# Layernorm by TensorE ahead of the first tile of an adjacency kernel, its first load issued earlier, and row blocks marked whole or not at all

## The chip, the cores and the metric

The kernel runs on one core of a Trainium2 chip. The metric is the device time of one launch in microseconds (us), the median of three runs. Beside it stands one profiled execution, whose span (first to last instruction) is what the trace divides up. Engines are called PE (TensorE; PEld is its weight load), DVE (VectorE), ACT (ScalarE), POOL (GpSimd) and SP (SyncE, which here only issues DMAs).

## The reference

```python
N, D_IN, D_OUT = (4096, 64, 64); MAX_NEIGH = 100; DECAY = 0.5
h = jnp.maximum(_layernorm(x, axis=-1), 0.0)        # x: 4096 x 64
support = h @ weight
mask = (adj != 0)                                   # adj: 4096 x 4096
rank = jnp.cumsum(mask, axis=1)
deg = rank[:, -1:]
k = jnp.minimum(deg, 100.)
pos = rank - (deg - k)
w = mask * jnp.where(pos > 0, 0.5 ** (k - pos), 0.0)
out = x + (w @ support + bias)
```

Every row of `adj` gives its nonzero columns weights that halve from the last nonzero backwards; those weights times a 4096 x 64 matrix, plus bias and x, are the result. `adj` is 64 MB in fp32 and is nearly all the data.

## The kernel before

**Tiles.** Row r of `adj` belongs to partition r // 32 and to tile r % 32, so there are 32 tiles of 128 rows. Column j belongs to partition j // 32 and to step t = j % 32 once PE has turned it. Tiles are taken in 18 units (`SIZES`): four of one tile (0, 1, 2, 17), fourteen of two.

**What a unit costs.** POOL loads a tile from fp32 to bf16 (`load`, L200 to 206, 1 MB in SBUF each) into a ring of 7 buffers. DVE turns it into a byte mask (`mask`, L310), adds halves of the mask (L316, three times, L344 the last) and scans the sums (L353), which gives for each run of columns how many nonzeros stand behind it. PE then begins a chain in PSUM (`base`, L549) and goes through the steps (`count`, L561 and L563), ACT turns each step's exponents into bit patterns of bf16 powers (`weigh`, L266), and PE multiplies them with the support rows into an accumulator (`product`, L570, 192 columns, since the support stands as three bf16 parts). DVE at the end adds the three parts, x and bias (`add_low`, `add_middle`, `add_high`), and SP stores.

**Marked or plain.** `MARKS[u]` says how many tiles of a unit are marked. A marked tile costs PE two matmuls a step and chain (`diag_own` and `diag_past`) and DVE nothing more. A plain tile costs PE one (`diag_step`), and DVE a maximum (`floor`, L362) and a difference (`differ`, L369) over each batch of 8 steps, on which that batch's products wait. 20 of the 32 tiles are marked in both kernels.

**Order.** Nothing schedules at run time. PE, ACT and DVE each go through slots g = 0, 1, 2 and so on, and do in each what tables place there: unit u begins in slot `STARTS[u]` (its base), counts in the next 8 or 16 slots, and its products come `LAGS[u]` slots behind. Chain c = u % 3 has one PSUM bank. A count of slot g+1 waits for the ACT instruction of slot g of its chain. DVE places the masks of a unit 9 and 7 slots ahead of its base, the halvings 6, 5 and 4, the scans 3 and 2 ahead. Each engine works in program order, so whatever waits holds all behind it.

**Layernorm.** Ahead of the slots DVE and POOL center x (`center`, L403 and L223), ACT squares (`square`, L239, into the last load buffer), DVE sums the squares (`square_sums`, L408), and between the DVE work for tiles 0 to 2 come the reciprocal deviation (L412 to 427) and the product with it (`normalize`, L432). PE turns the rows (`turn_h`, L514), ACT applies the Relu (L248), PE multiplies by the weight (`make_support`, L524), and ACT and PE split the result in three bf16 parts (`part`, L255; `take_off`, L532) in slots 5 to 11.

## Time and profile before

| | |
|---|---|
| median of 3 runs | 231.36 us (231.02 to 233.29) |
| the profiled execution | 232.5 us, of which the span is 230.1 us |
| PE busy | 201.8 us, 88% of the span, 2768 matmuls |
| DVE busy | 197.7 us, 86%, 227 instructions |
| ACT busy | 163.7 us, 71%, 303 instructions |
| DMA | 36.11 MB moved, about 216 GB/s from 6 to 165 us |
| first matmul | at 18.0 us |

A matmul's duration in the trace is its latency (its end is modelled), so the pace of PE is read from the starts of consecutive matmuls, or from how many there are in a stretch. The share of the DMA engines is that of 16 engines together. A number in square brackets at a row's end is the idle time ahead of it and what ended it.

### The profile page before, as it was taken

How to read it: one execution, taken by the hardware profiler on the slowest of the kernel's cores; microseconds unless marked ns; L12 is line 12 of the kernel's file. 1: busy time of each engine (PE TensorE's matmuls, PEld its weight loads, DVE VectorE, ACT ScalarE, POOL GpSimd, SP SyncE). 2: the span in 40 equal slices, each digit the busy share in tenths (PEclk: the TensorE clock that was granted, in tenths of full speed). 3: DMA queues.
4: the chain of work that ended last, by engine and by line, in shares of the span. 5: the costliest groups of instructions: out<-in, count | busy, mean ns of one | idle time of the engine just before them, and what ended most of it. 6: DMA issues, size and time to landing. Idle time of an engine off the chain costs nothing.

```text
span 230.1 us, 6364 instructions
## 1 busy us (share of the span) xinstructions
PE 201.8 (88%) x2768; PEld 196.3 (85%) x2768; DVE 197.7 (86%) x227; ACT 163.7 (71%) x303; POOL 26.0 (11%) x53
## 2 busy tenths in 40 slices
PE   0005898899999999999999999999999899899994
PEld 0004885899999999999999999999999789899993
DVE  1799999997799989999979999969999999677053
ACT  2203489767877988878887878887889798787610
POOL 8921000411000010110010001000000000000000
PEclk9999999999999999999999999999999999999999
DMA  5999999999999999999999999999700000000001
GB/s 182 227 214 194 215 216 216 216 216 216 212 215 216 215 214 211 215 219 216 215 215 219 218 214 220 212 218 218 158 20 3 11 3 14 0 14 3 11 14 29
DMA packets 8074, 36.11 MB, mean 157 GB/s; under 512 B 1648, under 2 KB 3440, under 8 KB 3952
## 3 DMA queue, kind: packets, MB, share of 16 engines
q0 software_dynamic: 4608, 33.56, 70.1%
q1 hardware_dynamic: 3136, 2.10, 3.5%
q8 instruction: 22, 0.36, 0.6%
q10 hardware_dynamic: 304, 0.07, 0.1%
q14 instruction: 4, 0.03, 0.0%
HBM read 68.22 MB, written 1.05 MB: 301 GB/s over the span
## 4 chain that ended last, share of the span: by engine, by line
PE 71%; DVE 17%; issue 4%; DMA 4%; ACT 3%; POOL 1%; POOLq 0%
PE acc L570 31%; PE chain L563 22%; PE chain L561 13%; DVE masks L310 6%; DMA adj_b<-in_adj 4%; DVE part L316 3%; DVE powers L369 2%; PE acc L524 2%; ACT support L255 2%; DVE powers L362 2%; PE chain L549 1%; PE acc L514 1%; ACT powers L266 1%; DVE later L353 1%; DVE sums L344 1%
## 5 line engine op out<-in xcount | busy, mean ns | idle before, releaser
L266 ACT ACTIVATE powers<-chain 128x512 int16<-128x512 f32 (+1 forms) x282 | 152.3, 568 | 39.3 <-PE chain L563 31.3
L570 PE MATMUL acc<-support,powers 128*128 128x192 bf16 x1024 | 167.5, 246 | 2.8 <-issue 1.3
L563 PE MATMUL chain<-diag_own,masks 128*128 128x128 bf16 x640 | 125.6, 231 | 0.0
L561 PE MATMUL chain<-diag_past,masks 128*128 128x128 bf16 x596 | 118.5, 224 | 3.0 <-ACT powers L266 2.9
L570 PEld LDWEIGHTS acc<-support,powers 128*128 128x128 bf16 x1024 | 101.1, 102 | 4.5 <-DVE powers L369 1.7
L563 PEld LDWEIGHTS chain<-diag_own,masks 128*128 128x128 fp8e3 x640 | 91.0, 147 | 0.0
L561 PEld LDWEIGHTS chain<-diag_past,masks 128*128 128x128 fp8e3 x596 | 84.8, 145 | 5.0 <-ACT powers L266 4.7
L310 DVE TENSOR_SCALAR masks<-adj_b 128x4096 uint8<-128x4096 bf16 x32 | 72.9, 2279 | 3.8 <-DMA adj_b<-in_adj 3.8
L563 PE MATMUL chain<-diag_step,masks 128*128 128x128 bf16 x384 | 62.2, 220 | 0.0
L563 PEld LDWEIGHTS chain<-diag_step,masks 128*128 128x128 fp8e3 x384 | 52.1, 145 | 0.0
L206 POOL DMA_DIRECT2D adj_b<-in_adj x32 | 18.7, 585 | 116.3 <-DVE masks L310 111.8
L369 DVE TENSOR_TENSOR powers<-powers 128x2048 bf16<-128x2048 bf16 (+1 forms) x20 | 28.5, 1423 | 0.0
L353 DVE TENSOR_TENSOR_SCAN later<-sums 128x257 bf16<-128x257 uint8 (+1 forms) x32 | 22.9, 721 | 0.4
L549 PE MATMUL chain<-diag_base,later 128*128 128x128 bf16 x68 | 7.1, 226 | 18.0 <-DVE later L353 18.0
L362 DVE TENSOR_SCALAR powers<-powers 128x2304 int16<-128x2304 int16 (+3 forms) x20 | 17.2, 862 | 6.2 <-ACT powers L266 6.2
L549 PEld LDWEIGHTS chain<-diag_base,later 128*128 128x128 bf16 x68 | 4.8, 103 | 18.0 <-issue 18.0
L316 DVE TENSOR_TENSOR part<-masks 128x2048 uint16<-128x2048 uint16 (+1 forms) x18 | 19.9, 1104 | 0.2
L379 DVE TENSOR_TENSOR sum_a<-acc,x_sb 128x128 f32<-128x128 f32 (+1 forms) x18 | 4.9, 272 | 12.0 <-PE acc L570 12.0
L344 DVE TENSOR_TENSOR sums<-part 128x512 uint16<-128x512 uint16 (+1 forms) x18 | 11.9, 663 | 0.5
L316 DVE TENSOR_TENSOR part<-part 128x1024 uint16<-128x1024 uint16 (+1 forms) x16 | 10.5, 654 | 0.1
L255 ACT ACTIVATE support<-acc 128x512 bf16<-128x512 f32 x12 | 6.8, 620 | 1.9 <-PE acc L524 1.9
L394 DVE TENSOR_REDUCE row_sum<-x_sb 128x16 f32<-128x1024 f32 x2 | 2.4, 1220 | 5.4 <-DMA x_sb<-in_x 5.4
(45 smaller groups left out, 53.0 us busy)
## 6 DMA issues: line engine op xcount, KB each, us to landing
adj_b<-in_adj POOLq DMA_DIRECT2D x32, 1024.0 KB, 30.3
x_sb<-in_x SPq DMA_DIRECT2D x2, 512.0 KB, 4.7
out<-x_sb SPq DMA_DIRECT2D x14, 64.0 KB, 2.6
out<-x_sb SPq DMA_DIRECT2D x4, 32.0 KB, 9.3
w<-in_L_gnn_weight ACTq DMA_DIRECT2D x2, 16.0 KB, 4.6
bias_b<-in_L_gnn_bias ACTq DMA_DIRECT2D x1, 32.0 KB, 4.5
```

The costliest lines, as they stand in the source:

```text
L206: pool.dma_start(adj_b[:, n % LOADS, :], adj_t[n]).then_inc(adj_loaded[n % LOADS], 16)
L266: nc.scalar.activation(powers[:, c, b, cols].bitcast(i16), chain[c][:, cols], ACT.Relu, bias=(MAX_NEIGH + 1) * STEP).then_inc(powers_ready ...
L310: nc.vector.tensor_scalar(masks[:, (n + SHIFT) % RING, :], adj_b[:, n % LOADS, :], 0.0, 1.0, ALU.not_equal, ALU.mult).then_inc(mask_ready, 1)
L316: return nc.vector.tensor_tensor(outs, at[:, :, 0:length], at[:, :, length:2 * length], ALU.add).then_inc(done, 1)
L344: nc.vector.tensor_tensor(runs_of(sums, sums_4, u)[:, :, 0:h * P], at[:, :, :, 0], at[:, :, :, 1], ALU.add).then_inc(sums_ready, 1)
L353: nc.vector.tensor_tensor_scan(runs_of(later, later_4, u)[:, k, ::-1], two[:, 0, ::-1], two[:, 1, ::-1], (OWN + STEP) / STEP if k < MARKS[ ...
L362: nc.vector.tensor_scalar(bits, bits, STEP, None, ALU.max).then_inc(floored[c], 1)
L369: nc.vector.tensor_tensor(before, before, after, ALU.subtract).then_inc(weights_ready[c], 1)
L549: last = nc.tensor.matmul(chain[c][:, at:at + P], behind[:, hs - 1 - h], diag_base[:, :], start=(k + h == 0), stop=False, skip_group_check ...
L561: nc.tensor.matmul(chain[c][:, at:at + P], column(n, t + 1), diag_past[:, :], start=False, stop=False, skip_group_check=True)
L563: return nc.tensor.matmul(chain[c][:, at:at + P], column(n, t), diag_own[:, :] if marked else diag_step[:, :], start=False, stop=True, ski ...
L570: return nc.tensor.matmul(acc[u % ACCS][:, k * 3 * D:(k + 1) * 3 * D], powers[:, u % FLIGHT, s + 1 if k < MARKS[u] else s, at:at + P], sup ...
```

## The change

1. **Loads.** POOL issues load 0 ahead of the constants and no longer centers half of x. The load ring has 8 buffers and the mask ring 12 (7 and 10 before); room for this comes from placing `cen` and `h_t` in the power buffer of chain 2 and the squares in that of chain 1. x comes in two halves as before, which now interleave in runs of four rows of 64 numbers (1 KB) and not of eight (2 KB).
2. **Layernorm.** PE runs 40 matmuls that nothing reads, and then, ahead of slot 0, turns the centered rows, not the normalized ones. ACT both squares and Relus them out of PSUM, and PE sums the squares by a matmul with two columns of ones. `make_support` works on relu(x - mean) in slot 1, into the four accumulator banks, and DVE multiplies by the reciprocal deviation there (`scale`), since relu(c r) = r relu(c) for r > 0. `square_sums` and `normalize` go. The three parts are taken in slots 1 to 6.
3. **DVE order.** `variance` comes behind `mask(1)`; the bias is added in four quarters at slots 15, 24, 50 and 72; the first scan of a unit comes in the slot of the last halving.
4. **Tables.** `MARKS`, `STARTS` and `LAGS` are new. The units with plain tiles were 4, 6, 7, 9, 10, 12, 13, 16 (one each) and 14, 15 (two); now they are 5, 16 (one) and 8, 11, 14, 15 (two).

`SIGNED` is empty, so the new `signs` and its branch in `mask` issue nothing.

```diff
-    LOADS = 7
-    RING = 10
+    LOADS = 8
+    RING = 12
-    MARKS = [1, 1, 1, 2, 1, 2, 1, 1, 2, 1, 1, 2, 1, 1, 0, 0, 1, 1]
-    STARTS = [0, 5, 10, 15, 22, 28, 33, 39, 45, 50, 56, 62, 67, 73, 79, 84, 90, 96]
-    LAGS = [14, 10, 8, 11, 11, 11, 11, 11, 11, 11, 11, 11, 11, 11, 11, 11, 11, 8]
+    MARKS = [1, 1, 1, 2, 2, 1, 2, 2, 0, 2, 2, 0, 2, 2, 0, 0, 1, 1]
+    STARTS = [0, 5, 7, 13, 22, 29, 34, 39, 46, 51, 56, 63, 68, 73, 80, 85, 90, 97]
+    LAGS = [7, 7, 8, 11, 11, 11, 11, 11, 11, 11, 11, 11, 11, 11, 11, 11, 11, 7]
...
-                if n == LOADS - 1:
-                    pool.wait_ge(sq_sum_ready, 2)
...
             nc.gpsimd.memset(w2[:, :], 0.0).then_inc(w2_zeroed, 1)
+            load(0)
             for m in (ident_f, minus, diag_own, diag_past, diag_step, diag_base):
...
-            pool.wait_ge(mean_ready, 2)
-            nc.gpsimd.tensor_tensor(half_of(cen, 1), half_of(x_sb, 1), spread(mean, 1),
-                                    ALU.subtract).then_inc(cen_ready[1], 1)
...
+            def scale(i):
+                dve.wait_ge(ln_step, 6)
+                dve.wait_ge(support_ready, i + 1)
...
+                nc.vector.tensor_tensor(block_of, block_of, of_block.unsqueeze(3).to_broadcast([P, RUNS, 2, D]),
+                                        ALU.mult).then_inc(scaled[i], 1)
...
+            def keep_warm(times):
+                for _ in range(times):
+                    nc.tensor.matmul(chain[0][:, 0:P], minus[:, :], diag_step[:, :], start=True, stop=True,
+                                     skip_group_check=True)
+            def sum_squares(i):
+                pe.wait_ge(sq_ready, i + 1)
+                for q in range(4):
+                    t = 8 * q + 6 - 2 * i
+                    last = nc.tensor.matmul(sq_sum[:, t:t + 2], sq_t[:, 4 * i + q, :], pair_sum[:, :],
+                                            start=(q == 0), stop=True, skip_group_check=True)
...
             pe.wait_ge(consts_ready, 6)
+            keep_warm(40)
+            turn_h(0)
+            turn_h(1)
+            pe.wait_ge(consts_ready, 7)
+            sum_squares(0)
+            turn_h(2)
+            sum_squares(1)
+            turn_h(3)
+            sum_squares(2)
+            sum_squares(3)
             for g in range(SLOTS):
...
+                if g == 1:
+                    make_support(0)
+                    make_support(1)
+                    make_support(2)
+                    make_support(3)
...
-                    if u >= 3 and to == 3:
+                    if u >= 3 and to == 4:
                         scan(u, 0)
```

On DVE, at the start of the program, these rows stood before (row sums of x, the first mask, the squares' sums):

```order
L394 TENSOR_REDUCE row_sum<-x_sb 128x2x8 x2
L398 TENSOR_SCALAR mean<-row_sum 128x2x8 x2
L403 TENSOR_TENSOR cen<-x_sb,mean 128x2x512
L408 TENSOR_REDUCE sq_sum<-adj_b 128x2x8
L310 TENSOR_SCALAR masks<-adj_b 128x4096
L316 TENSOR_TENSOR part<-masks 128x1024
L408 TENSOR_REDUCE sq_sum<-adj_b 128x2x8
L344 TENSOR_TENSOR sums<-part 128x512
L353 SCALAR_TENSOR_TENSOR later<-sums 128x513
L412 TENSOR_SCALAR var_eps<-sq_sum 128x32
L310 TENSOR_SCALAR masks<-adj_b 128x4096
```

In the changed kernel there stand (L445 is `center`, which writes where the powers will be; L450 is `variance`, which reads a chain's bank):

```order
L436 TENSOR_REDUCE row_sum<-x_sb 128x4x4
L445 TENSOR_TENSOR powers<-x_sb,mean 128x4x256
L440 TENSOR_SCALAR mean<-row_sum 128x4x4
L445 TENSOR_TENSOR powers<-x_sb,mean 128x4x256
L351 TENSOR_SCALAR masks<-adj_b 128x4096
L357 TENSOR_TENSOR part<-masks 128x1024
L385 TENSOR_TENSOR sums<-part 128x512
L394 SCALAR_TENSOR_TENSOR later<-sums 128x513
L351 TENSOR_SCALAR masks<-adj_b 128x4096
L450 TENSOR_SCALAR var_eps<-chain 128x32
```

Nothing of layernorm stands between the first mask and its scan any more, both halves are centered on DVE, and the variance has moved behind the second mask.

On ACT, from the square root on, the rows of the changed kernel are these (L262 is `root`, L298 `weigh`, L275 `part`):

```order
L262 ACTIVATE std<-var_eps 128x32
L298 ACTIVATE powers<-chain 128x512
L275 ACTIVATE support<-acc 128x4x2x64 x2
L298 ACTIVATE powers<-chain 128x512
L275 ACTIVATE support<-acc 128x4x2x64 x2
L298 ACTIVATE powers<-chain 128x512
L275 ACTIVATE support<-acc 128x4x2x64 x2
```

Before, four `weigh` came directly behind the root, and no part ahead of the sixth:

```order
L243 ACTIVATE std<-var_eps 128x32
L266 ACTIVATE powers<-chain 128x512 x4
L248 ACTIVATE h_t<-acc 128x512 x2
L266 ACTIVATE powers<-chain 128x512
L255 ACTIVATE support<-acc 128x8x64 x2
L266 ACTIVATE powers<-chain 128x512
```

So the parts now alternate with unit 0's steps from the first step on.

On DVE, where units 14 and 15 (both plain) are at work, the rows before were:

```order
L362 TENSOR_SCALAR powers<-powers 128x4608
L353 SCALAR_TENSOR_TENSOR later<-sums 128x257
L369 TENSOR_TENSOR powers<-powers 128x4096
L379 TENSOR_TENSOR sum_a<-acc,x_sb 128x128
L362 TENSOR_SCALAR powers<-powers 128x8x256
L384 TENSOR_TENSOR sum_b<-acc,sum_a 128x128
L316 TENSOR_TENSOR part<-masks 128x1024
L369 TENSOR_TENSOR powers<-powers 128x8x256
```

and are now:

```order
L403 TENSOR_SCALAR powers<-powers 128x4608
L410 TENSOR_TENSOR powers<-powers 128x4096
L421 TENSOR_TENSOR sum_a<-acc,x_sb 128x128
L426 TENSOR_TENSOR sum_b<-acc,sum_a 128x128
L357 TENSOR_TENSOR part<-masks 128x1024
L431 TENSOR_TENSOR x_sb<-acc,sum_b 128x128
L385 TENSOR_TENSOR sums<-part 128x512
L394 SCALAR_TENSOR_TENSOR later<-sums 128x513
```

The scan between maximum (L362, now L403) and difference (L369, now L410) has moved ahead of them, and unit 13's maximum and difference over 256 columns are gone.

## Rows read from the trace of the kernel before

**Rows 1.** Busy time by stretch: us, each engine's busy us (x instructions), clock, DMA, GB/s
```profile
150.00:160.00 10.00, 10.00 (x150) 10.00 (x148) 8.21 (x12) 8.19 (x15) 0.00 (x0) 1.00 1.04 217
...
180.00:190.00 10.00, 8.55 (x121) 8.26 (x121) 9.90 (x11) 8.21 (x16) 0.00 (x0) 1.00 0.03 8
190.00:200.00 10.00, 9.12 (x133) 8.98 (x132) 8.34 (x11) 8.26 (x15) 0.00 (x0) 1.00 0.03 8
```

**Rows 2.** The chain of work that ended last: start us, us, what
```profile
35.05 2.04 PE acc L524 x16
...
43.18 0.22 PE chain L549 x4
...
73.10 0.22 PE chain L549 x4
...
226.79 0.30 DVE sum_a L379
```

**Rows 3.** Timeline of DVE at the start: start us, us, instruction, idle before
```profile
11.82 2.31 DVE L310 TENSOR_SCALAR masks<-adj_b 128x4096 uint8<-128x4096 bf16 x1 [0.29 <-DMA adj_b<-in_adj]
...
14.78 1.21 DVE L408 TENSOR_REDUCE sq_sum<-adj_b 128x16 f32<-128x1024 f32 x1
...
16.62 1.23 DVE L353 TENSOR_TENSOR_SCAN later<-sums 128x513 bf16<-128x513 uint8 x1
17.76 0.15 DVE L412 TENSOR_SCALAR var_eps<-sq_sum 128x32 f32<-128x32 f32 x1
```

**Rows 4.** Timeline: the first DMA issues of x (SP) and of adj (POOL)
```profile
0.74 1.27 SPq L189 DMA_DIRECT2D x_sb<-in_x  x2
...
3.54 2.27 POOL L206 DMA_DIRECT2D adj_b<-in_adj  x4
```

**Rows 5.** DMA queues, 5 to 6 us: packets, MB, share; q1 moves x, q0 adj
```profile
q1 hardware_dynamic: 165, 0.31, 80.5%
q0 software_dynamic: 7, 0.06, 27.9%
```

**Rows 6.** DMA queues, 61 to 62 us; q1 now stores 32 KB of the output
```profile
q0 software_dynamic: 28, 0.20, 93.8%
q1 hardware_dynamic: 28, 0.01, 5.1%
```

**Rows 7.** Timeline of ACT: the first `weigh`, and two `part`
```profile
19.05 0.60 ACT L266 ACTIVATE powers<-chain 128x512 int16<-128x512 f32 x1 [0.86 <-PE chain L563]
...
39.08 1.13 ACT L255 ACTIVATE support<-acc 128x512 bf16<-128x512 f32 x2
```

**Rows 8.** Timeline of DVE: bias over 2 x 1024 columns, tile 4, tile 10
```profile
32.33 2.35 DVE L438 TENSOR_TENSOR x_sb<-x_sb,bias_b 128x1024 f32<-128x1024 f32 x2
34.72 2.29 DVE L310 TENSOR_SCALAR masks<-adj_b 128x4096 uint8<-128x4096 bf16 x1
...
39.77 1.28 DVE L353 TENSOR_TENSOR_SCAN later<-sums 128x257 bf16<-128x257 uint8 x2
...
62.78 2.29 DVE L310 TENSOR_SCALAR masks<-adj_b 128x4096 uint8<-128x4096 bf16 x1 [1.42 <-DMA adj_b<-in_adj]
```

**Rows 9.** Timeline of PE, slot 19: its first matmuls, and the first of slot 20
```profile
49.25 0.24 PE L570 MATMUL acc<-support,powers 128*128 128x192 bf16 x1
49.33 0.22 PE L561 MATMUL chain<-diag_past,masks 128*128 128x128 bf16 x1
49.39 0.23 PE L563 MATMUL chain<-diag_own,masks 128*128 128x128 bf16 x1
...
51.02 0.24 PE L570 MATMUL acc<-support,powers 128*128 128x192 bf16 x1
```

**Rows 10.** Timeline of DVE at unit 14: maximum, unit 16's second scan, difference
```profile
185.48 1.36 DVE L362 TENSOR_SCALAR powers<-powers 128x4608 int16<-128x4608 int16 x1
186.76 0.69 DVE L353 TENSOR_TENSOR_SCAN later<-sums 128x257 bf16<-128x257 uint8 x1
187.36 2.27 DVE L369 TENSOR_TENSOR powers<-powers 128x4096 bf16<-128x4096 bf16 x1
```

More of the change, by code:

```diff
@@ L216, in _ @@
                                         pattern=[[-1, P]], channel_multiplier=1).then_inc(consts_ready, 1)
-            for n in range(4):
+            nc.gpsimd.affine_select(out=pair_sum[:, :], in_=pair_sum[:, :], compare_op=ALU.is_ge, fill=0.0, base=0,
+                                    pattern=[[-D, 2]], channel_multiplier=1).then_inc(zeroed, 1)
+            pool.wait_ge(zeroed, 8)
+            nc.gpsimd.affine_select(out=pair_sum[:, :], in_=pair_sum[:, :], compare_op=ALU.is_ge, fill=0.0, base=D - 1,
+                                    pattern=[[D, 2]], channel_multiplier=-1).then_inc(consts_ready, 1)
+            for n in range(1, 4):
                 load(n)
@@ L246, in turn_h, with part, signs @@
                 act.wait_ge(h_turned, i + 1)
-                t = 4 * BLOCKS[i]
-                nc.scalar.activation(h_t[:, t:t + 4, :], turned[i % 2][:, :].rearrange("p (a b) -> p a b", a=4),
+                nc.scalar.activation(h_t[:, 4 * i:4 * i + 4, :], turned[i % 2][:, :].rearrange("p (a b) -> p a b", a=4),
                                      ACT.Relu).then_inc(h_t_ready, 1)
-            def part(i, s, ready):
-                act.wait_ge(split_ready, 6 * (i // 2) + 2 * s + i % 2 + 1)
-                t = 8 * BLOCKS[i]
-                nc.scalar.activation(support[:, t:t + 8, s, :], split[i % 2][:, :].rearrange("p (t d) -> p t d", d=D),
-                                     ACT.Copy).then_inc(ready, 1)
+            def part(i, s):
+                if s:
+                    act.wait_ge(part_taken[i], s)
+                else:
+                    act.wait_ge(scaled[i], 1)
+                nc.scalar.activation(steps_of(support[:, :, s, :], i),
+                                     split[i][:, :].rearrange("p (r two d) -> p r two d", two=2, d=D),
+                                     ACT.Copy).then_inc(part_ready[i], 1)
+            def signs(n, j):
+                act.wait_ge(adj_loaded[n % LOADS], 16 * (n // LOADS + 1))
+                if n >= RING:
+                    u = UNIT_OF[n - RING]
+                    act.wait_ge(chain_ready[u % FLIGHT], taken_until(u) + TAKEN[u])
+                at = slice(j * N // PIECES, (j + 1) * N // PIECES)
+                nc.scalar.activation(masks[:, (n + SHIFT) % RING, at].bitcast(i8), adj_b[:, n % LOADS, at],
+                                     ACT.Sign).then_inc(signs_ready, 1)
             def weigh(u, b):
@@ L264, in weigh @@
                 act.wait_ge(chain_ready[c], taken_until(u) + b + 1 - (MARKS[u] == SIZES[u]))
+                if u in (1, 2) and b <= 1:
+                    act.wait_ge(sq_sum_ready if u == 1 else support_ready, 4)
                 cols = slice(0, SIZES[u] * CHAINS[u] * P) if b else plain(u)
@@ L300, in _ @@
                             weigh(u, g - STARTS[u])
+                for n in SIGNED:
+                    if 0 <= g - SIGNED[n] < PIECES:
+                        signs(n, g - SIGNED[n])
+                if g == 1:
+                    part(0, 0)
+                    part(1, 0)
+                if g == 2:
+                    part(2, 0)
+                    part(3, 0)
+                if g == 3:
+                    part(0, 1)
+                    part(1, 1)
+                if g == 4:
+                    part(2, 1)
+                    part(3, 1)
+                if g == 5:
+                    part(0, 2)
+                    part(1, 2)
+                if g == 6:
+                    part(2, 2)
+                    part(3, 2)
         @block.vector
@@ L305, in mask @@
             def mask(n):
+                if n in SIGNED:
+                    dve.wait_ge(signs_ready, PIECES * (1 + sum(m < n for m in SIGNED)))
+                    two = masks[:, (n + SHIFT) % RING, :].bitcast(u16)
+                    nc.vector.tensor_scalar(two, two, 0x0101, None, ALU.bitwise_and).then_inc(mask_ready, 1)
+                    return
                 dve.wait_ge(adj_loaded[n % LOADS], 16 * (n // LOADS + 1))
@@ L453, in _ @@
             scan(0, 0)
+            mask(1)
             variance()
-            mask(1)
             halve_1(1)
             deviation()
+            scale(0)
             halve_2(1)
+            scale(1)
             halve_3(1)
             scan(1, 0)
-            normalize(0)
+            scale(2)
+            scale(3)
             mask(2)
             halve_1(2)
-            normalize(1)
             halve_2(2)
```

192 lines of the change are left out of this document (89 added, 103 removed).

## The prediction

> **What bounds the kernel now.** I read the busy time by stretch first. From 150 to 160 us PE starts 150 matmuls, 15 a us [rows 1]. Elsewhere two things fall out of that pace: 180 to 200 us has 121 and 133 matmuls where 300 would fit [rows 1], so (300 - 254) / 15 = 3.1 us are lost there; and up to about 50 us PE is thin.
>
> Then I read where the slots lie in time, by the bases in the chain of waits: unit 3's base (slot 15) is at 43.18, unit 6's (slot 33) at 73.10, and the last adds begin at 226.79 [rows 2]. The prediction is made in these three pieces.
>
> Then the timeline inside a slot. A product is 0.08 us, a count 0.06 [rows 9]. Slot 19 lasts 51.02 - 49.25 = 1.77 us with 24 matmuls, which are 1.5 us of work [rows 9]. The rest is the round trip: a chain's 12 matmuls (0.80 us) and then about 0.95 us until ACT's result is back. So a slot lasts the greater of PE's work and (matmuls of its busiest chain + 0.95): 1.42 us for a chain with eight counts, 1.75 with four products besides. By this rule the 18 slots from 43.18 to 73.10 should take 29.6 us, and took 29.9.
>
> Last, DMA. Tile 10's mask began only when its load landed, at 62.78 [rows 8]. The adj stream is continuous, so how early it starts and what stands behind it matter.
>
> **The start.** DVE took the first mask at 11.82, when load 0 had landed, and the scan that releases PE began at 16.62 and took 1.23 [rows 3]. The square sum at 14.78 (1.21) in between goes [rows 3]: the scan ends at 16.7, 1.15 earlier than 17.85. I give nothing for issuing load 0 earlier. x was issued at 0.74, adj at 3.54 [rows 4], and from 5 to 6 us x still fills 80% of the engines while adj gets its first 7 packets [rows 5]: x and load 0 together need the engines until about 11.5 whoever goes first. Both ends: nothing, or 1 us for gaps in the x phase that adj fills. The worse end is a rival below.
>
> Centering the second half on DVE costs 1.2 us of DVE, between x's landing and 11.8 us where DVE idled; the transposes, squares and their sums lie in PE's and ACT's idle time ahead of the slots. The 40 matmuls (0.11 us each at the low level of TensorE's clock is 4.3 us, an estimate by doubling the 0.06 of [rows 9]) start when the constants are there, about 4.2 us, and end before the centered rows are ready at about 9. If x is on time they cost nothing; if the clock is up for the first slots they gain little, because those slots are set by ACT, as follows.
>
> **Slots 0 to 12.** The gain of 1.15 is given back at once. `variance` was at 17.76 [rows 3] and is now behind `mask(1)`: 16.7 + 2.25 = 19.0. ACT's root stands ahead of the first `weigh`, so that one is at about 19.4, and was at 19.05 [rows 7]. Behind it ACT waits for `scale(0)`: halving 0.7, the six small operations 1.25, scale about 0.6 (half of a bias instruction of 1024 columns, 2.35 / 2 [rows 8]), so 21.7 us. Its operand is in PSUM; twice that price would put 0.6 us more before each of the first scales, 1 to 2 us in all, and I keep that for the range. PE meanwhile does all of `make_support`, 2 x 2.04 us by [rows 2], until about 22.
>
> From 21.7 ACT has two parts (1.13 [rows 7]) and a `weigh` (0.60 [rows 7]) in each slot, 1.7 us, with two short waits for scales 1 to 3 (0.9 us together). That puts slot 7 at about 31.5. Slots 7 and 8 have unit 0's eight counts and four products (1.75 each), ACT is 0.1 behind in them, slots 9 to 12 are light (1.18 three times, 1.35). Unit 3's base, now slot 13, comes at 31.5 + 3.6 + 4.9 = **40.0**, against 43.18.
>
> A bound from DVE stands just below. Tile 4's mask at 34.72 was 6.3 us ahead of the end of unit 3's scans, 39.77 + 1.28 [rows 8]. Tiles 0 and 10 landed at 11.82 and 62.78 at the latest [rows 3, 8], 5.1 us a load; tile 4's is then there at 32.2 at best, and the base not before 38.5. The early part can't gain more than 4.7.
>
> **Slots 13 to 33.** Unit 6's base is now slot 34, so this piece has 21 slots and not 18. By the rule: slot 13 1.35, slot 14 1.5, nine of 1.42 (unit 3's or 4's eight counts alone), six of 1.75 (slots 24 to 29, unit 3's products beside its counts), three of 1.42 and one of 1.75. That is 32.2 us, for 29.9 before: the earlier start is half spent on more and emptier slots. Unit 6's base comes at 72.2, for 73.10. Again DMA is close: tile 10 can't be masked before 62.78, and mask, three halvings, scan, another mask and scan (2.2 + 1.4 + 0.7 + 0.7 + 0.6 + 2.2 + 1.0) give a base not before 71.6.
>
> **From unit 6's base on.** Before, 226.8 - 73.1 = 153.7. The matmuls left behind it are 892 products and 1280 counts for 902 and 1226: +0.8 us after pricing all. The marks: six units' 12 maxima and 12 differences over one tile become 6 and 6 over two. On DVE that saves the fixed cost of twelve instructions and leaves the elements as they were; it is off the path, and I put it at nothing. What counts is the 3.1 us lost at 180 to 200. There the maximum at 185.48 (1.36) and the difference at 187.36 (2.27) had a scan of 0.69 between them [rows 10], and unit 13's plain tile stood in the same queue. Both are gone; DVE has the difference done before the third slot behind (3.6 us for some 5.4). I take 3.0 of the 3.1 back, and charge 0.5 for units 8 and 11, now plain, where a bias quarter or a halving still stands between the two. 153.7 + 0.8 - 3.0 + 0.5 = 152.0.
>
> **Sum.** 40.0 + 32.2 + 152.0 = 224.2, for 226.8: 2.6 us less of the profiled span of 230.1, which becomes 227.5. The profiled execution took 232.5, the median is 231.36, and I take the difference off the median: **228.8 us**.
>
> **Rivals.** *x is starved by load 0 (slower).* In the first us of [rows 6] 28 packets of each queue went: an adj packet of 8 KB for each of 256 bytes, one by one, in turn. If the turns hold from the moment adj's packets come, now about 2.2 us behind an issue at 1 us (as before from 3.54 to the end of the stretch of [rows 5]), x's 1 KB packets go one to each 0.6 us of an engine. Nearly all of x is still to move then. Against it: at 5 to 6 us x had 165 packets to adj's 7 [rows 5], and the packets of adj began only as x ran out, as if what is already handed to an engine goes first. How much of x is handed over by 3.2 us no row shows. If a third of it isn't, its last 20 packets on each engine take 20 x 0.62 = 12 us, it lands near 16 instead of soon after 6, DVE reaches mask 0 at 19 instead of 11.8, and the end moves by 7: 231.36 + 4.7 = 236. If most isn't, it takes the loads' own time: 250 or more. Decision point: x complete later than 8.5 us, since DVE then reaches mask 0 after 11.8, and each us costs one. The Trainium skill, "DMA: Bandwidth & Descriptors", section "Queues, rings and completion order", says that each DMA engine takes the queues in turn, one packet after another. By that rule x is starved; the trace agrees at 61 us and not at 5 us. Chance 0.28, a third of it for the worst.
>
> *The early gain is given back (no change).* The scales' PSUM price, ACT's alternation, or DVE falling behind on plain units 8 and 11 (floor and difference of two tiles, 3.6 us, ahead of everything else) costs 1.5 us more: 230.3. For it: DVE is busy 9.90 of 10 us where plain units were at work [rows 1]. Against: layernorm's share of DVE shrinks, four instructions of 1.2 us going for one and four scales of 0.6. Chance 0.27.
>
> *The clock and DMA give more.* Adj lands a us earlier by filling x's gaps and slots 1 to 6 run at the round trip, not ACT's pace: base 3 at 39, and no stall late: 227.3. It belongs to the forecast's side.
>
> **Chances.** The forecast, gain of 1 to 4 us, 0.45; the no-change case 0.27; starved 0.28. Predicted 228.8, its own range 226.8 to 230.3. The whole range reaches to the milder starved case: 226.5 to 237; a tenth is left above. About 1% (2.3 us) is what a measurement of this kernel can tell from no change. Faster by more than that needs below 229.05: most of the forecast's own case, 0.45 with the better rival in it; same 0.29; slower 0.26.
>
> **What would show it.** The first mask at 11.5 to 11.9 and x's second row sum ahead of 7.5 us: no starving. A second row sum behind 8.5 us: the rival. The first scan ending at 16.7, the root at 19.1 and the first `weigh` at 19.4. ACT without gaps from 22 to 32. Unit 3's base at 40, unit 6's at 72 with tile 10's mask still waiting for its load. 180 to 200 us with nearly 300 matmuls. The forecast is wrong if unit 3's base is later than 42, or if PE falls under 14 matmuls a us around units 8 and 11.

## The result, and the profile of the changed kernel

| | before | changed |
|---|---|---|
| median | 231.77 us (231.02 to 233.29, 4 runs) | 249.59 us (248.31 to 250.17, 4 runs) |
| ratio to before | | 1.075, 95% interval 1.068 to 1.083 |
| span of the profiled execution | 230.1 us | 247.5 us |
| slot 0 begins on PE | 17.99 us | 40.44 us |
| PE busy, matmuls | 201.8 us, 2768 | 216.1 us, 2900 |
| DVE busy, instructions | 197.7 us, 227 | 192.1 us, 214 |

The forecast was 228.8 us (226.5 to 237.0). The kernel became 7.5% slower, and its time lies above the whole range. The first rival, x starved by load 0, came true, near its worst form ("250 or more").

One correction to what stands ahead of the prediction. It is not 20 of 32 tiles that are marked in both kernels: the new `MARKS` marks 22, so 10 tiles are plain and not 12. The forecast added matmuls for this (1280 counts for 1226 behind unit 6's base; the trace has 1266), but its sentence on DVE was wrong: 20 maxima and 20 differences became 12 and 12, over fewer elements as well. The page of the changed kernel has 1680 counts behind the first step of each unit and base (704 + 656 + 320), before it had 1620 (640 + 596 + 384).

These are rows of the page of the changed kernel: the granted clock in 40 slices, the chain's shares by engine, one group of instructions, and one DMA issue (x, with its median time from issue to landing):

```profile
PEclk9955555999999999999999999999999999999999
...
PE 83%; DMA 11%; ACT 3%; DVE 1%; issue 1%; SPq 0%
...
L436 DVE TENSOR_REDUCE row_sum<-x_sb 128x16 f32<-128x1024 f32 x2 | 2.4, 1220 | 23.7 <-DMA x_sb<-in_x 23.7
...
x_sb<-in_x SPq DMA_DIRECT2D x2, 512.0 KB, 15.0
```

DVE's two row sums waited 23.7 us for x, and x took 15.0 us in the median of its halves. All later reading starts from that. Next, parts of the chain of work that ended last (start, duration, what):

```profile
1.49 26.31 DMA x_sb<-in_x
...
27.82 1.22 DVE row_sum L436
...
30.23 1.12 PE spare L567 x4
...
37.37 3.21 PE chain L575 x16
40.58 0.45 PE chain L609 x4
41.02 0.43 PE chain L623 x4
41.45 4.86 PE acc L583 x32
```

It begins with the load of x, goes over the second row sum to PE's turns and square sums (L567, L575), and only at 40.58 to the first base. DVE in the same stretch (start, duration, instruction, idle before):

```profile
27.82 1.22 DVE L436 TENSOR_REDUCE row_sum<-x_sb 128x16 f32<-128x1024 f32 x1 [19.21 <-DMA x_sb<-in_x]
...
31.43 2.29 DVE L351 TENSOR_SCALAR masks<-adj_b 128x4096 uint8<-128x4096 bf16 x1
...
35.20 1.23 DVE L394 TENSOR_TENSOR_SCAN later<-sums 128x513 bf16<-128x513 uint8 x1
...
40.61 0.19 DVE L450 TENSOR_SCALAR var_eps<-chain 128x32 f32<-128x32 f32 x1 [2.00 <-PE chain L575]
```

The second row sum stood at 6.62 us before. Load 0 had landed at about 10 us, but tile 0's mask still began only at 31.43, because it stands behind the centering in DVE's program order. Then I looked at the packets. Of the DMA queues, q1 moves x and q0 adj (packets, MB, share of 16 engines); first from 3 to 4 us, then from 4 to 5:

```profile
q1 hardware_dynamic: 361, 0.36, 101.5%
q0 software_dynamic: 6, 0.05, 24.8%
```

```profile
q0 software_dynamic: 26, 0.21, 102.0%
q1 hardware_dynamic: 11, 0.01, 1.8%
```

Within one us x fell from 361 packets to 11. When adj's first packet began, at 3.89 us, 485 of x's 1024 data packets had begun, so about 34 were left on each of the 16 engines. From 12 to 13 us it was still one for one, and the last of x came in at 27.4 us. The stretch from 12 to 13:

```profile
q0 software_dynamic: 18, 0.15, 85.3%
q1 hardware_dynamic: 19, 0.02, 7.3%
```

Windows of the changed kernel (columns as in [rows 1]):

```profile
20.00:30.00 10.00, 0.00 (x0) 0.00 (x0) 2.18 (x2) 0.00 (x0) 0.00 (x0) 0.50 1.05 224
...
150.00:160.00 10.00, 10.00 (x151) 10.00 (x150) 9.71 (x12) 8.21 (x15) 0.72 (x2) 1.00 1.01 211
...
200.00:210.00 10.00, 10.00 (x146) 9.86 (x145) 8.88 (x10) 9.02 (x17) 0.00 (x0) 1.00 0.03 8
210.00:220.00 10.00, 10.00 (x147) 9.92 (x146) 7.04 (x9) 9.58 (x18) 0.00 (x0) 1.00 0.03 8
```

From 20 to 30 us nothing ran on PE or ACT. Late in the kernel the pace of nearly 15 a us holds; 200 to 220 us is the work of 180 to 200 in the kernel before, shifted by the late start. So the loss is all at the start. PE's timeline says the same: slot 13 begins at 60.72, slot 34 at 92.47, and the last adds come at 244.16. From slot 13 to 34 it took 31.75 us and from there to the last adds 151.7, within 0.5 us of the forecast's 32.2 and 152.0.

### The profile page after: what moved, and what is told of

It reads as the page before. It is cut to its first block, busy times and chain, and to the rows that moved or that the text cites. A ratio compares the mean times of both kernels' runs of the same rounds, so it can differ in the third digit from the quotient of the medians.

```text
span 247.5 us, 6684 instructions
## 1 busy us (share of the span) xinstructions
PE 216.1 (87%) x2900; PEld 209.8 (85%) x2900; DVE 192.1 (78%) x214; ACT 161.7 (65%) x301; POOL 29.3 (12%) x55
## 4 chain that ended last, share of the span: by engine, by line
PE 83%; DMA 11%; ACT 3%; DVE 1%; issue 1%; SPq 0%
PE acc L630 35%; PE chain L623 25%; PE chain L621 15%; DMA x_sb<-in_x 11%; PE chain L575 3%; PE acc L583 2%; ACT support L275 2%; PE chain L609 2%; ACT powers L298 1%; PE spare L567 1%; PE chain L567 1%; DVE row_sum L436 0%; DVE powers L445 0%; SPq L204 0%; DVE sum_a L421 0%
## 5 line engine op out<-in xcount | busy, mean ns | idle before, releaser
L298 ACT ACTIVATE powers<-chain 128x512 int16<-128x512 f32 (+1 forms) x278 | 150.4, 572 | 38.0 <-PE chain L623 35.9
L623 PE MATMUL chain<-diag_own,masks 128*128 128x128 bf16 x704 | 132.0, 227 | 0.0
L621 PE MATMUL chain<-diag_past,masks 128*128 128x128 bf16 x656 | 125.2, 222 | 0.8 <-ACT powers L298 0.5
L623 PEld LDWEIGHTS chain<-diag_own,masks 128*128 128x128 fp8e3 x704 | 98.3, 146 | 0.0
L621 PEld LDWEIGHTS chain<-diag_past,masks 128*128 128x128 fp8e3 x656 | 92.1, 145 | 3.5 <-ACT powers L298 3.2
L623 PE MATMUL chain<-diag_step,masks 128*128 128x128 bf16 x320 | 49.0, 220 | 0.0
L623 PEld LDWEIGHTS chain<-diag_step,masks 128*128 128x128 fp8e3 x320 | 43.0, 144 | 0.0
L219 POOL DMA_DIRECT2D adj_b<-in_adj x32 | 24.3, 764 | 130.2 <-DVE masks L351 129.2
L403 DVE TENSOR_SCALAR powers<-powers 128x4608 int16<-128x4608 int16 (+3 forms) x12 | 13.4, 1114 | 21.4 <-ACT powers L298 21.4
L410 DVE TENSOR_TENSOR powers<-powers 128x4096 bf16<-128x4096 bf16 (+1 forms) x12 | 23.2, 1931 | 0.2
L436 DVE TENSOR_REDUCE row_sum<-x_sb 128x16 f32<-128x1024 f32 x2 | 2.4, 1220 | 23.7 <-DMA x_sb<-in_x 23.7
L567 PE MATMUL spare<-ident_f,powers 128*128 128x128 f32 x8 | 2.2, 432 | 21.0 <-DVE powers L445 21.0
L567 PEld LDWEIGHTS spare<-ident_f,powers 128*128 128x128 f32 x8 | 1.6, 241 | 21.2 <-DVE powers L445 21.2
L557 PE MATMUL chain<-diag_step,minus 128*128 128x128 bf16 x40 | 4.4, 313 | 4.8 <-POOL minus L230 4.8
```

What stands on the lines that cost most here:

```text
L219: pool.dma_start(adj_b[:, n % LOADS, :], adj_t[n]).then_inc(adj_loaded[n % LOADS], 16)
L298: nc.scalar.activation(powers[:, c, b, cols].bitcast(i16), chain[c][:, cols], ACT.Relu, bias=(MAX_NEIGH + 1) * STEP).then_inc(powers_ready ...
L403: nc.vector.tensor_scalar(bits, bits, STEP, None, ALU.max).then_inc(floored[c], 1)
L410: nc.vector.tensor_tensor(before, before, after, ALU.subtract).then_inc(weights_ready[c], 1)
L567: last = nc.tensor.transpose(turned[i % 2][:, q * P:(q + 1) * P], pairs_of(cen[:, :, :], i)[:, q, :], ident_f[:, :])
L621: nc.tensor.matmul(chain[c][:, at:at + P], column(n, t + 1), diag_past[:, :], start=False, stop=False, skip_group_check=True)
```

## The experiments

Theory S (starved): adj's packets take turns with x's, one for one, so x is late by the packets it still has to move on each engine, times the time of an adj packet; all else of the forecast holds. The rival theory: it is not the order of the loads but the new layernorm (longer chain on PE, slower scale, cold clock) or the tables. Unless another is named, an edit is against the changed kernel. Kernel 1 is the kernel of experiment 1, and so on. Ratios are to the kernel before, timed beside it on the same chip; x is complete when its last packet has begun.

**1. Load 0 behind the constants, everything else of the change kept.**

```diff
-            load(0)
...
-            for n in range(1, 4):
+            for n in range(4):
                 load(n)
```

> The changed kernel with load 0 issued behind the constants again, all else as changed. Theory T (load 0's packets take turns with the second half of x, which landed at 27.4 us for about 6): x complete at 6 to 7 us, the first mask at about 12, unit 3's base 20.3 us behind unit 0's, so near 38, unit 6's at 70, and the time 249.6 - 21 + up to 1 = 228 to 230 us. Rival L (layernorm on TensorE ahead of the slots, with the clock at its low level, is what costs): time stays above 238 us, since the prelude's chain from the second row sum to slot 0 is kept (12.6 us in the changed kernel). Rival P (1 KB packets of x are slow in themselves): x lands later than 8 us even so.

Measured: 229.16 us (228.85 to 229.65), ratio 0.984 (0.980 to 0.988), span 227.0. x was complete at 6.20 us. The place of one DMA issue in POOL's order is worth 20 us. The time was inside the expected range, the bases of units 3 and 6 came 2 us later than the 38 and 70 expected. DVE, PE's chain and ACT of this kernel, in three views:

```profile
13.07 2.29 DVE L350 TENSOR_SCALAR masks<-adj_b 128x4096 uint8<-128x4096 bf16 x1 [2.15 <-DMA adj_b<-in_adj]
...
16.85 1.23 DVE L393 TENSOR_TENSOR_SCAN later<-sums 128x513 bf16<-128x513 uint8 x1
...
22.38 0.70 DVE L472 TENSOR_TENSOR acc<-acc,rstd 128x512 f32<-128x512 f32 x1 [0.24 <-PE acc L582]
...
63.04 2.29 DVE L350 TENSOR_SCALAR masks<-adj_b 128x4096 uint8<-128x4096 bf16 x1 [1.22 <-DMA adj_b<-in_adj]
```

```profile
9.49 0.86 PE spare L566 x4
...
16.38 3.20 PE chain L574 x16
19.58 0.45 PE chain L608 x4
```

```profile
20.39 0.23 ACT L261 ACTIVATE std<-var_eps 128x32 f32<-128x32 f32 x1 [2.89 <-DVE var_eps L449]
20.53 0.58 ACT L297 ACTIVATE powers<-chain 128x512 int16<-128x512 f32 x1
23.11 0.60 ACT L274 ACTIVATE support<-acc 128x512 bf16<-128x512 f32 x1 [2.00 <-DVE acc L472]
```

This kernel lets the forecast be read without the starved x. In PE's timeline its bases of unit 3 and unit 6 came at 39.98 and 72.04 (forecast 40.0 and 72.2):

```profile
39.98 0.33 PE L608 MATMUL chain<-diag_base,later 128*128 128x128 bf16 x3
...
72.04 0.34 PE L608 MATMUL chain<-diag_base,later 128*128 128x128 bf16 x3
```

**2. The kernel before, with load 0 ahead of the constants and nothing else.**

```diff
             nc.gpsimd.memset(w2[:, :], 0.0).then_inc(w2_zeroed, 1)
+            load(0)
...
-            for n in range(4):
+            for n in range(1, 4):
```

> The kernel before with nothing changed but load 0 ahead of the constants; x still in 2 KB packets. Theory T, turns packet by packet: the second half of x has 17 packets an engine and not 33, so it lands 17 x 0.65 = 11 us behind 4.1, near 15.5 us, against about 6; the second row sum is at 15.5 and the time 231.8 + 8 to 10 = 240 to 242 us. Rival L or P: x lands near 6 us as before, and the time is within 1 us of 231.8. A turn of equal bytes and not of packets would make x land as late as in the changed kernel, 27 us, and cost 18.

Measured: 242.88 us (242.11 to 243.61), ratio 1.043 (1.038 to 1.047). The old kernel starves as well, so none of the rest of the change is needed for the loss. Its x goes in packets of 2 KB, half as many, and was complete at 17.5 us, 2 us later than I had expected; the time is 0.9 us above the expected 240 to 242. The second row sum, and then the queues from 12 to 13 us:

```profile
18.00 1.22 DVE L395 TENSOR_REDUCE row_sum<-x_sb 128x16 f32<-128x1024 f32 x1 [11.17 <-DMA x_sb<-in_x]
```

```profile
q0 software_dynamic: 21, 0.17, 85.8%
q1 hardware_dynamic: 22, 0.05, 13.2%
```

One packet for one again, whether x's are 1 or 2 KB. The extra delay over 6.2 us is 21.2 us with 1 KB and 11.3 with 2 KB. When adj's first packet began, about 34 KB of x were left on an engine in the changed kernel, and about 40 KB here (20 packets, since 188 of 512 had begun by 4.10 us). More bytes and fewer packets gave the smaller delay, so it goes with the number of x's packets, not with its bytes.

**3. Load 0 first, x in one DMA of 8 KB a partition (8 packets on each engine for 64).**

```diff
-            for f in range(2):
-                sp.dma_start(half_of(x_sb, f), half_of(x.rearrange("(p t) d -> p t d", t=T), f))\
-                  .then_inc(x_loaded[f], 16)
+            sp.dma_start(x_sb[:, :, :], x.rearrange("(p t) d -> p t d", t=T)).then_inc(x_loaded[0], 16)
...
-                dve.wait_ge(x_loaded[f], 16)
+                dve.wait_ge(x_loaded[0], 16)
```

> The changed kernel, load 0 first as changed, but x in one DMA of 8 KB a partition, so 8 data packets an engine for 64. Theory T: its packets start at about 2.2 us and load 0's at 3.8; at most some 4 or 5 packets an engine are left and take turns with adj: x lands at 4 + 5 x 0.9 = 8 us or less, and the time is 228 to 231 us. If adj's load starves x whatever the packets, it lands later than 15 us. Rival L: above 238 us.

Measured: 228.01 us (227.70 to 228.71), ratio 0.980 (0.976 to 0.984), span 225.9. Load 0 is issued as early as in the changed kernel, and x was complete at 5.20 us. With the time between two issues left alone and x put into one DMA of larger packets, 21.6 us of the changed kernel's span are gone. DMA from 4 to 5 us, and DVE:

```profile
q1 hardware_dynamic: 49, 0.37, 87.3%
q0 software_dynamic: 4, 0.03, 16.3%
```

```profile
15.05 1.23 DVE L392 TENSOR_TENSOR_SCAN later<-sums 128x513 bf16<-128x513 uint8 x1
17.03 2.29 DVE L349 TENSOR_SCALAR masks<-adj_b 128x4096 uint8<-128x4096 bf16 x1 [0.75 <-DMA adj_b<-in_adj]
```

The result is the expected one, but its means are not. Adj's first packet came at 4.91 us, 1.0 later than in the changed kernel, and by then all 128 packets of x had begun, so here there were no turns to take. It shows that few large packets avoid the loss; it doesn't test the price of a turn. Why adj's first packet came later isn't shown. The turns themselves are shown by the changed kernel's packets, by 2 and by 8. Whether an early load 0 is worth anything stays open here; 9 and 10 below are for that.

**4. Kernel 1 without `keep_warm(40)`.**

> As the run with load 0 behind the constants, but without the 40 matmuls that nothing reads. If they raise the clock for the transposes and sums: those are at the low level without them, 1 to 2 us longer in the prelude, but this lies in time in which load 0 is awaited, so the total is the same within 0.5 us. If the prelude is on the path, the total is 1 to 2 us more.

Measured: 229.40 us (228.75 to 229.88), ratio 0.985 (0.981 to 0.989), against 0.984: in this kernel the 40 matmuls are worth nothing that can be measured. The row's granted clock differs, the work doesn't. From 12 to 16 us, first kernel 1 with the 40 matmuls, then the one without, then kernel 3, which has them as well:

```profile
12.00:16.00 4.00, 4.00 (x21) 4.00 (x22) 2.90 (x2) 1.54 (x3) 0.34 (x1) 0.50 1.02 213
```

```profile
12.00:16.00 4.00, 4.00 (x21) 4.00 (x21) 2.93 (x2) 1.85 (x4) 0.37 (x1) 1.00 1.01 211
```

```profile
12.00:16.00 4.00, 3.90 (x36) 3.82 (x35) 3.90 (x4) 2.86 (x6) 0.54 (x1) 1.00 0.91 166
```

That is not all that can be said of them. In kernel 1 the 40 matmuls end at 7.4 us and the turns begin at 9.49, and the turns and square sums run at the low level. In kernel 3 they end at 9.3, the turns begin at 9.93, and PE stays at the high level until about 16.5: it begins 36 matmuls in this stretch for 21, its last 16 square sums take 1.90 us for 3.41, and slot 0 begins at 16.33. No run takes the 40 matmuls out of kernel 3, so what they are worth there isn't shown.

**5. Kernel 3 with the marks of before** (20 marked tiles, not 22), starts as changed.

```diff
-    MARKS = [1, 1, 1, 2, 2, 1, 2, 2, 0, 2, 2, 0, 2, 2, 0, 0, 1, 1]
+    MARKS = [1, 1, 1, 2, 1, 2, 1, 1, 2, 1, 1, 2, 1, 1, 0, 0, 1, 1]
```

> Load 0 first, x in one DMA (228.0 us, 0.980 of before), but with the marks of the kernel before: 20 marked tiles and 12 plain for 22 and 10. PE has 60 counts fewer, 3.5 us of its work. Theory M (the new marks pay by keeping DVE ahead where units 14 and 15 are): the plain tiles' maxima and differences cost stalls as in 180 to 200 us before, 3 us, so the total is 0 to 1 us off 228.0 either way, with stalls late and fewer matmuls. Rival W (PE's work alone decides): 3.5 us less, 224.5. Rival D (DVE falls behind throughout): 2 us or more above 228.

Measured: 235.94 us (234.54 to 237.10), ratio 1.017 (1.013 to 1.022), 8 us more than kernel 3, with 60 matmuls fewer on PE (rival D). PE now waits for DVE's differences. From the waits (engine, line, waited for: us, times, longest) and the page:

```profile
PE acc L628 <- DVE powers L408: 5.2, 5, 1.8
```

```profile
PE 211.8 (91%) x2840; PEld 204.8 (88%) x2840; DVE 198.2 (85%) x230; ACT 163.2 (70%) x305; POOL 23.8 (10%) x55
```

DVE's 198.2 us of work are 8 more than kernel 3's 190.3. But those starts were made for other marks, so the size of this is not that of the marks; hence 11.

**6. Kernel 3 with `variance` ahead of `mask(1)`.**

```diff
-            mask(1)
             variance()
+            mask(1)
```

> Load 0 first, x in one DMA, and variance ahead of mask 1 as in the kernel before. If the first weigh waits for the root, and that for mask 1, as the prediction had it: the root comes 2.2 us earlier, the scales too, slots 2 to 12 begin up to 2 us earlier, and the total is 226 to 227 us, unless unit 3's base is then held by tile 4's load (landed 31.9, so base 3 not before 38.2, for 38.65 now): in that case the gain is 0.5 us at most.

Measured: 228.65 us (228.03 to 230.10), ratio 0.987 (0.983 to 0.991). No gain, and the expectation missed. The variance came at 16.81 for 19.24 in kernel 3, but slot 2 began at 23.0 for 22.06 and slot 13 at 39.2 for 38.65. DVE:

```profile
16.81 0.19 DVE L448 TENSOR_SCALAR var_eps<-chain 128x32 f32<-128x32 f32 x1 [0.53 <-PE chain L573]
17.18 2.30 DVE L349 TENSOR_SCALAR masks<-adj_b 128x4096 uint8<-128x4096 bf16 x1 [0.18 <-DMA adj_b<-in_adj]
```

It had to wait for PE's square sums, and the mask that it was moved past began 0.15 us later. What sets slot 2 is not the root but `make_support` in slot 1, which doesn't wait for the root: 4.9 us in kernel 3 (17.12 to 22.06). That slot 2 came a us later is PE's pace and not the order: `make_support` began 0.3 us later and took 5.6 us (17.44 to 23.02). From 16 to 20 us the granted clock was 0.50 here and 0.57 in kernel 3, and it was back at 1.00 at 21.5 us here, at 19.9 there. So this run does not show by itself what an earlier variance is worth.

**7. Load 0 between POOL's zeroing and its selects.**

```diff
-            load(0)
             for m in (ident_f, minus, diag_own, diag_past, diag_step, diag_base):
                 nc.gpsimd.memset(m[:, :], 0.0).then_inc(zeroed, 1)
             nc.gpsimd.memset(pair_sum[:, :], 1.0).then_inc(zeroed, 1)
+            load(0)
```

> The changed kernel (x in halves of 1 KB packets) with load 0 behind POOL's memsets but ahead of its selects, about 1 us later than changed and 1.7 us earlier than behind all. Theory T, turns packet by packet from the moment load 0's packets come (4.7 to 5 us): x's second half, 33 packets an engine at 0.045 us from 4.1, has about 15 to 20 out by then; the other 13 to 18 take 0.65 each, so x lands at 13 to 17 us and the time is 236 to 240. If packets already handed to the engine go first, x lands by 7 us and the time is 228 to 229.

Measured: 232.4 us, from two runs (230.19 and 234.60) that lie too far apart for a ratio; only the order of the DMAs is read, from the trace of the longer one. Both times are below the expected 236 to 240, and x was complete at 12.29 us, a little ahead of the expected 13 to 17 and far behind kernel 1's 6.20. The first adj packet came at 5.34 us, only 0.1 us ahead of kernel 1's (5.44). But from 5 to 6 us adj began 14 packets here and 3 there, and from 6 to 7 us 21 and 10, and x had about 8 packets an engine left for about 4. What decides is what of x is left in the queue when adj's packets come in number, and there the edge is steep.

**8. The changed kernel, but loads 1 and on wait for all of x.**

```diff
+            pool.wait_ge(x_loaded[1], 16)
             for n in range(1, 4):
                 load(n)
```

> The changed kernel, load 0 first, but loads 1 and on wait for the whole of x. Theory T: the second half of x takes turns with load 0 alone, 9 packets an engine, and then has the engines to itself: it lands at 10 to 11.5 us for 27.4, mask 0 begins at about 15, and the time is 231 to 233 us. If it is load 0 itself that holds x up and not the turns with all that follow, x lands as late as 20 us or more.

Measured: 233.62 us (232.87 to 234.17), ratio 1.007 (1.004 to 1.011). x was complete at 11.36 us, one and a half us after load 0 (9.9): x shares the engines with load 0 alone, and is free when that is done. Tile 0's mask:

```profile
11.71 1.22 DVE L437 TENSOR_REDUCE row_sum<-x_sb 128x16 f32<-128x1024 f32 x1 [5.75 <-DMA x_sb<-in_x]
...
16.66 2.42 DVE L352 TENSOR_SCALAR masks<-adj_b 128x4096 uint8<-128x4096 bf16 x1
```

It came 1.7 us later than the expected 15, and the time is 0.6 us over the expected range. So in the changed kernel it was loads 1 to 3, queued behind load 0, that kept x waiting from 10 to 27 us.

**9. The kernel before with load 0 first (as 2) and x whole (as 3).**

> The kernel before, with load 0 issued ahead of the constants and x in one DMA of 8 KB packets: what the early load alone is worth where it doesn't starve x. Theory (small packets starve): x lands near 5.2 us as in the changed kernel with x whole, load 0 near 10.3, mask 0 at about 11.3 for 11.82, and the end 0.5 to 1 us earlier than before: 230.4 to 231.4, no measurable change. Rival: x whole makes DVE's two row sums and centers start later (one wait for all of x) and costs more than the load gives: 232 or more.

Measured: 231.78 us (231.29 to 232.20, 12 runs) beside 232.25, ratio 0.9976 (0.9965 to 0.9987). The early load and x whole together are worth 0.5 us here, the lower end of what I expected; this run doesn't part the two.

**10. Kernel 3 with load 0 behind the constants** (kernel 1 with x whole).

> The changed kernel with load 0 behind the constants and x in one DMA: beside the run with x in halves (229.16) it gives what x whole is worth, beside the run with load 0 first and x whole (228.01) what the early load is worth. Theory: the 1.1 us between those two is the early load, so this one comes at 229.0 to 229.4, with slot 0 near 19.4. Rival: it is x's fewer packets that let load 0 land earlier, and the place of the load is worth nothing: 228.0 to 228.4, slot 0 near 16.5.

Measured: 227.92 us (227.76 to 228.33), ratio 0.981 (0.979 to 0.983), the same as kernel 3's 0.980 within the intervals. The expected 229.0 to 229.4 missed and the rival's time came just below its range: the early load is worth nothing, and the 1.2 us between 1 and 3 go with x's fewer packets. But the rival was not right in its means, since slot 0 began at 18.05 and not at 16.5. Tile 0's scan ended 0.9 us later than in kernel 3, and PE's square sums, which ran at a granted 0.50 from 14 us on and at 1.00 there, ended another 0.9 us behind it. DVE shows why both come out equal all the same:

```profile
12.16 2.29 DVE L348 TENSOR_SCALAR masks<-adj_b 128x4096 uint8<-128x4096 bf16 x1 [1.27 <-DMA adj_b<-in_adj]
...
15.94 1.23 DVE L391 TENSOR_TENSOR_SCAN later<-sums 128x513 bf16<-128x513 uint8 x1
17.09 2.27 DVE L348 TENSOR_SCALAR masks<-adj_b 128x4096 uint8<-128x4096 bf16 x1
```

Tile 0's mask is 0.9 us later than in kernel 3 (12.16 for 11.28), tile 1's is not (17.09 for 17.03), since load 1 landed at 16.7 in both. An early load 0 takes from load 1 what it gains, and unit 3 begins at 38.80 for 38.65.

**11. Kernel 3 with the marks of before and, from unit 4 on, the starts of before.**

```diff
-    MARKS = [1, 1, 1, 2, 2, 1, 2, 2, 0, 2, 2, 0, 2, 2, 0, 0, 1, 1]
+    MARKS = [1, 1, 1, 2, 1, 2, 1, 1, 2, 1, 1, 2, 1, 1, 0, 0, 1, 1]
-    STARTS = [0, 5, 7, 13, 22, 29, 34, 39, 46, 51, 56, 63, 68, 73, 80, 85, 90, 97]
+    STARTS = [0, 5, 7, 13, 22, 28, 33, 39, 45, 50, 56, 62, 67, 73, 79, 84, 90, 96]
```

> Load 0 first and x whole, with the marks of before and, from unit 4 on, the very starts of before (units 0 to 3 as in the changed kernel). The run with the old marks on the new starts took 235.94. If those 8 us came from starts that don't fit the marks, this one gives them back: from unit 6's base on it takes 153 to 154 us as before did, and since slot 33 can't come earlier than tile 10 lets it, the end is near 226 to 227 and the time 230 to 231.5. If plain tiles cost DVE that much whatever the starts, it stays above 234.

Measured: 232.81 us (232.13 to 234.20, 12 runs), ratio 1.002 (1.000 to 1.004). Neither expectation held. 3 of the 8 us of experiment 5 were the starts that didn't fit; 4.8 us stay between this kernel and kernel 3, and they are the marks with starts made for them. The windows, first of this kernel, then of kernel 3:

```profile
180.00:190.00 10.00, 8.57 (x124) 8.32 (x123) 9.90 (x11) 8.01 (x15) 0.00 (x0) 1.00 0.03 8
190.00:200.00 10.00, 8.72 (x122) 8.38 (x123) 9.77 (x13) 8.29 (x16) 0.00 (x0) 1.00 0.02 7
```

```profile
180.00:190.00 10.00, 10.00 (x146) 9.86 (x144) 8.88 (x10) 9.13 (x18) 0.00 (x0) 1.00 0.03 8
190.00:200.00 10.00, 10.00 (x147) 9.92 (x146) 7.08 (x8) 9.07 (x17) 0.00 (x0) 1.00 0.03 7
```

With the old marks the thin stretch of [rows 1] is back: (300 - 246) / 15 = 3.6 us lost, against (300 - 293) / 15 = 0.5. DVE has work for 9.9 and 9.8 of 10 us there, and for 8.9 and 7.1 with the new marks. Another loss is at 68 to 74 us, where PE waited 2.8 us for a scan, ahead of unit 6's base, with DVE busy all the 6 us. Behind this wait the granted clock was 0.50 from 72.9 to 76.3 us, and PE began 28 matmuls in these 3.4 us where 15 a us would be 51, so 1.5 us are lost there. From unit 6's base to the last adds it took 156.2 us, and 153.9 before in the same view. Why DVE is behind at 68 us I haven't taken apart.

## Why the prediction failed, step by step

**The step that failed** is in "The start": "x and load 0 together need the engines until about 11.5 whoever goes first", from which I gave "nothing for issuing load 0 earlier", with x landed soon after 6 us. That is right for load 0 and x taken together, and wrong for x, on which everything in DVE's queue hangs: x was complete at 27.4 us. I saw the mechanism, gave it 0.28, and gave the worst form, which came, a third of that. My decision point, x complete later than 8.5 us, was passed by 19 us. Against it I set 5 to 6 us before the change, with 165 packets of x to 7 of adj [rows 5], and read it "as if what is already handed to an engine goes first". The row allowed another reading: at that time x was nearly through, it ended at 6.25 us by the trace, and adj's first packets came only from 5.6 us on. There was next to nothing left to take turns with. The row at 61 us, 28 to 28 [rows 6], was the one that showed both queues with work, and so the one to go by. By it, the estimate could have been made: half of x is 32 packets an engine of 1 KB, behind each stands an adj packet of about 0.6 us, so some 20 us beyond 4 us, not the 12 us of my "third". The trace has 27.4 - 3.9 = 23.5 for 34 packets, 0.69 us each: an adj packet and one of x's, 0.06 us. The Trainium skill, "DMA: Bandwidth & Descriptors", section "Queues, rings and completion order", says that an engine takes its queues in turn, a packet at a time, and that such a packet is typically some 9 to 17 descriptors. The trace agrees on the turns and not on their size: a turn is here one data packet as the profile counts them, of 1 or 2 KB, against one of adj's 8 KB (19 to 18 in the changed kernel, 22 to 21 in kernel 2). The measurement decides.

Also wrong was the rival's milder case, "if a third of it isn't": more than half was still to go when adj's packets began (about 34 of 64 packets an engine).

**Where the 17.4 us of span went.** x 21.2 us later than before (27.43 for 6.25). In PE's timeline slot 0 is 22.45 us later, unit 3's base 17.7 (60.72 for 43.02) and unit 6's base 19.5 (92.47 for 72.94), and the last adds are 17.4 later. So the later slots gained back what the forecast said they would, on top of a start that had lost 22.

**The rest of the forecast**, read in kernel 1, where x is on time:

| step | forecast | kernel 1 |
|---|---|---|
| first mask | 11.8 | 13.07 |
| first scan's end | 16.7 | 18.08 |
| slot 0 on PE | 16.7 | 19.44 |
| root; first `weigh` | 19.1; 19.4 | 20.39; 20.53 |
| scale of one bank | 0.6 | 0.70 |
| unit 3's base | 40.0 | 39.98 |
| tile 10's mask, waits for its load | 62.78 at the earliest | 63.04, waited 1.22 |
| unit 6's base | 72.2 | 72.04 |
| last adds | 224.2 | 223.72 |

- *First mask:* 1.3 us late, because load 0 landed at 12.7 and not 11.4. POOL issued it 0.5 us later than before (4.01 for 3.54), and with x whole, issued at the same place, the load lands at 11.8 (kernel 10). That x's packets cost adj time by their number stood in no step of mine.
- *PE's part ahead of slot 0:* I said that turns and square sums "lie in PE's and ACT's idle time". They took from 9.49 to 19.58, and end 1.4 us behind the scan. The 32 square sums alone, two columns each, are 1.77 + 1.50 + 3.20 = 6.5 us. The step missed is a price for a matmul of two columns with fp32 weights: 0.2 us at the low level of the clock, 0.12 at the high one (16 in 1.90 us in kernel 3). In the changed kernel PE's work ended 4.0 us behind the scan (40.4 for 36.4), and these us are on the path. In kernels 3 and 10 it costs nothing later on, as tile 1 isn't there before 17.
- *Slots 0 to 12:* the late start was hidden. Slot 2 begins at 25.4 and slot 7 at 32.7 (forecast 31.5), then slots 7 to 12 take 7.3 us where I had 8.5. Two errors of 1.2 us cancelled, so that 39.98 for 40.0 is luck in part: the start was late, and the slots behind were lighter than my rule.
- *Slots 13 to 33:* 32.06 for 32.2. The rule of a slot (PE's work, or the busiest chain plus 0.95) held in sum.
- *From unit 6's base on:* 151.7 for 152.0, but not by the terms. "+0.8 us" for the matmuls doesn't follow from my own prices: 54 counts more at 0.06 and 10 products fewer at 0.08 are 2.4 us. The trace has 1266 counts and 884 products, 40 more and 18 fewer than before, and by these prices +1.0. And the 0.5 us charged for units 8 and 11 isn't seen: from 80 to 130 us kernel 1 begins 148 to 153 matmuls in each 10 us.
- *180 to 200 us:* "nearly 300 matmuls" came: 293 in kernel 3, and 293 at 200 to 220 in the changed kernel. I had put it on the scan no longer standing between the maximum and the difference, and the marks' saving on DVE "at nothing". Kernel 11 has a scan between them again (its tables decide that), so the two can't be told apart by it; what it shows is that marks with their starts make it. With 8 us less DVE work (198.2 in kernel 5, 190.3 in kernel 3) in an engine that was busy 9.9 of 10 us, "nothing" has no support.
- *The rival "given back", by DVE falling behind at the plain units,* didn't come true with the new tables. It did with the old marks (5 and 11).
- *`keep_warm`:* priced at nothing, measured at nothing where the clock fell before the square sums (4); not measured where it stayed up (kernel 3).

In all, what I called the forecast's case is 227.9 to 229.2 us (kernels 1, 3, 10). The sum was within 1 us, in part by terms that cancelled, and the gain is larger than the forecast's 1.1% (1.6 to 2.0%), since the kernel before took 232.3 to 232.9 us beside these runs. The chance was on the wrong case.

Kernels 3 and 10 beat both kernels: 0.980 (0.976 to 0.984) and 0.981 (0.979 to 0.983) of before, by about 4.5 us. Kernel 10 gives up the early load and loses nothing.

## What to carry to other kernels

In this case a DMA issued earlier delayed another that was already under way on the same engines. While both had packets waiting they took turns by packets, so the one with many small packets waited for the large packets of the other, as often as it had packets left. Before a load is moved ahead, count the packets per engine that the load everything waits for still has to move at that time, and multiply by the other's packet time; then make those packets larger or keep the order. And when two rows of a trace disagree on whether queues share, ask in which of them both really had work.

A cost table such as the marks is judged with its starts and not alone: the old marks cost 8 us on the new starts, and 4.8 on starts made for them.

## What the runs showed of the hardware that I had not expected

- With load 0 issued first and the bytes of x the same, x was complete at 27.4 us in 64 packets an engine of 1 KB, at 17.5 in 32 of 2 KB, and at 5.2 in 8 of 8 KB. In the first two it took turns with adj; in the third all of x had begun before adj's first packet.
- The 0.1 us in adj's first packet between kernels 7 and 1 (5.34 and 5.44) goes with 12.3 against 6.2 us for x. Adj's packets also came in faster in kernel 7 (14 for 3 from 5 to 6 us); no run separates the two.
- x in small packets also costs adj's stream: load 0 landed at 12.7 us with x in halves of 1 KB packets and at 11.8 with x whole, and the stream kept that lead.
- A matmul of 128x128 fp32 weights by two columns took 0.2 us (16 in 3.20 us, kernel 1) at the low level of TensorE's clock, and 0.12 (16 in 1.90 us, kernel 3) at the high level.
- The granted clock of a row can't be read as the pace of the engine while it has hardly worked. In kernel 4 the row has 1.00 from 12 to 16 us and in kernel 1 0.50, with 21 matmuls begun in each. In both, the four counts of slot 0 take 0.43 us in the chain, as in the changed kernel at a granted 0.50; later ones take 0.06 each.
